# Coefficients of four groups at once on GpSimd, normalisation 6:2, every fourth mask on ScalarE, weights loaded behind x's first tile, matmuls on zeros in TensorE's gaps

## What is computed

```
h   = relu((x - mean) / sqrt(var + 1e-5))            x: [128 graphs, 128 nodes, 128]
out = 0
for each direction (fwd, bwd, loop):
    p = h @ W.T;  g = p @ Wg.T
    vals_r = (p + b_r) * sigmoid(g + bg_r)           for each relation r of the direction
    out   += sum_r (adj == r) @ vals_r               (adj transposed for bwd and loop)
result = x + relu(out)
```

## Time and profile before

| | us |
|---|---|
| median of three runs | 113.24 |
| lowest, highest | 112.27, 114.36 |
| profiled execution | 112.11 |
| its span | 110.3 |
| busy in the span: TensorE, VectorE, ScalarE, GpSimd | 98.8, 94.0, 91.8, 87.1 |

### The profile page before, as it was taken

One profiled execution on the slowest core, in us unless ns is written; L12 is line 12 of the kernel. 1 busy time (PEld: TensorE's weight loads), 2 busy tenths in 40 slices (PEclk: granted clock), 3 DMA queues, 4 the chain that ended last, 5 costly groups with the idle time before them and its releaser, 6 DMA issues.

```text
span 110.3 us, 2526 instructions
## 1 busy us (share of the span) xinstructions
PE 98.8 (90%) x780; PEld 92.1 (83%) x780; DVE 94.0 (85%) x202; ACT 91.8 (83%) x153; POOL 87.1 (79%) x182
## 2 busy tenths in 40 slices
PE   5524789899999999999999999999999999999970
PEld 1113569789999999999999999999999999999960
DVE  1508529899999999999999999999999999897780
ACT  4137533999999999999999999999999999999650
POOL 2380790999999999999999999999999999995000
PEclk9999999999999999999999999999999999999999
DMA  2999999999999999999999999980606050515067
GB/s 73 281 311 281 286 290 291 292 291 292 291 317 311 343 332 321 320 320 321 305 320 301 260 309 274 317 222 6 190 6 190 6 180 10 158 38 176 14 185 207
DMA packets 50275, 25.48 MB, mean 231 GB/s; under 512 B 850, under 2 KB 50260, under 8 KB 50260
## 3 DMA queue, kind: packets, MB, share of 16 engines
q1 hardware_dynamic: 49968, 25.17, 81.6%
q10 hardware_dynamic: 292, 0.13, 0.5%
HBM read 16.91 MB, written 8.39 MB: 229 GB/s over the span
## 4 chain that ended last, share of the span: by engine, by line
PE 80%; DMA 5%; POOL 3%; DVE 3%; issue 2%; ACT 2%; ACTq 1%; DVEq 0%; POOLq 0%
PE psum L750 23%; PE psum L715 16%; PE psum L728 14%; PE psum L729 13%; PE psum L733 13%; DMA w_raw<-in_L_gnn_Wg_loop 5%; POOL rstd L309 1%; DVE x_all L560 1%; DVE stats L500 1%; POOL xn L324 1%; PE psum L691 1%; ACT xn L393 1%; ACT hT_hi L404 1%; ACT L374 1%; PE psum L688 0%
## 5 line engine op out<-in xcount | busy, mean ns | idle before, releaser
L728 PE MATMUL psum<-w_hi,hT_hi 128*128 128x256 f32 x128 | 35.1, 307 | 1.8 <-issue 0.8
L750 PE MATMUL psum<-vals,mask 128*128 128x128 f32 x256 | 33.6, 275 | 0.0
L411 ACT ACTIVATE psum<-bias_all 128x1024 f32<-128x1024 f32 x32 | 32.9, 1027 | 0.1
L324 POOL TENSOR_SCALAR xn<-x_all,mean_neg,rstd 128x128 f32<-128x128 f32 x75 | 32.8, 449 | 0.1
L729 PE MATMUL psum<-w_lo,hT_hi 128*128 128x256 f32 x128 | 32.4, 285 | 0.0
L750 PEld LDWEIGHTS psum<-vals,mask 128*128 128x128 f32 x256 | 31.2, 191 | 0.1
L728 PEld LDWEIGHTS psum<-w_hi,hT_hi 128*128 128x128 f32 x128 | 24.7, 193 | 2.8 <-issue 1.7
L309 POOL TENSOR_TENSOR rstd<-var_eps,minus_half 128x8 f32<-128x8 f32 (+1 forms) x17 | 26.6, 1564 | 0.0
L500 DVE BATCH_NORM_STATS2 stats<-x_all 128x6 f32<-128x256 f32 x64 | 23.9, 416 | 2.7 <-DMA x_all<-in_x 2.7
L535 DVE TENSOR_TENSOR vals<-psum,gate 128x512 f32<-128x512 f32 (+1 forms) x33 | 21.7, 659 | 4.3 <-ACT gate L426 4.2
L729 PEld LDWEIGHTS psum<-w_lo,hT_hi 128*128 128x128 f32 x128 | 24.8, 193 | 0.0
(11 more groups left out here) (34 smaller groups left out, 34.2 us busy)
## 6 DMA issues: line engine op xcount, KB each, us to landing
adj_all<-in_adj SPq DMA_DIRECT2D x16, 512.0 KB, 6.6
x_all<-in_x SPq DMA_DIRECT2D x15, 512.0 KB, 6.7
out<-x_all SPq DMA_DIRECT2D x15, 512.0 KB, 4.4
x_all<-in_x SPq DMA_DIRECT2D x2, 256.0 KB, 3.1
out<-x_all SPq DMA_DIRECT2D x1, 256.0 KB, 2.5
out<-x_all SPq DMA_DIRECT2D x2, 128.0 KB, 2.5
w_raw<-in_L_gnn_W_loop ACTq DMA_DIRECT2D x1, 64.0 KB, 3.2
w_raw<-in_L_gnn_Wg_loop ACTq DMA_DIRECT2D x1, 64.0 KB, 5.3
```

What stands on the lines that cost most here:

```text
L324: last = pool.tensor_scalar(xn[:, s, j * D:j * D + D], x_all[:, g * GC + j * D:g * GC + j * D + D], mean_neg[:, p, k:k + 1], rstd[:, p, k: ...
L411: nc.scalar.activation(prod_ps[s].rearrange("p g a d -> p g (a d)"), bias_all[:, :, :].rearrange("p a d -> p (a d)").unsqueeze(1) .to_broa ...
L728: nc.tensor.matmul(to, hi, w_hi[:, :], start=False, stop=False, skip_group_check=True)
L750: last = nc.tensor.matmul(to[:, j * D:j * D + D], mask[:, g % MASKS, j * N:j * N + N], vals[:, s, j * D:j * D + D], start=True, stop=True)
```

## The change

- Coefficients: `BATCHES` says which groups get theirs together: group 0, group 1, groups 2 and 3, 4 and 5, then four groups at a time from 6 on (16 columns). The slots for statistics and coefficients are four. shift is gone, and VectorE's tiles take the mean straight from the statistics (subtract, then multiply).
- Normalisation: ScalarE has no share. GpSimd has three tiles of each group and VectorE one (in the first two groups one and three), so 6 and 2 of the eight tiles of two groups.
- Masks: groups 0, 1 and every g with g % 4 == 3 are cast on ScalarE, in the loop two before; the others on GpSimd as before.
- Loads: W_loop and Wg_loop are issued from SP's queue right behind x's first group.
- TensorE: `keep_busy` makes matmuls on zeros, 16 in all, at five places of the start.
- VectorE: output before normalise in a loop; row_stats of group t+8 instead of t+6, so groups 7 and 8 are done before the loops too; normalise(0) stands ahead of the splitting of the weights.
- ScalarE's start: seed(0) stands ahead of the second half of w_hi, seed(1) behind relu_turned(0), the masks of groups 0 and 1 behind relu_turned(1).
- The store of the first half of the last group is issued from ScalarE.

```diff
+    BATCHES = [(0, 0), (1, 1), (2, 3), (4, 5)] + [(g, min(g + 3, GROUPS - 1)) for g in range(6, GROUPS, 4)]
+    BATCH = 4 * GROUP
...
-        def shares(g):
-
-            if g < 2:
-                return range(0), range(0, 2), range(2, 4)
-            if g % 2 == 0:
-                return range(0, 3), range(3, 4), range(4, 4)
-            return range(0, 2), range(2, 3), range(3, 4)
-
-        def act_norms(g):
-
-            return g + 1 if g < 2 else 2 + (g - 1) // 2
+        def batch_of(g):
+
+            for b, (first, last) in enumerate(BATCHES):
+                if first <= g <= last:
+                    return b, first, last
+
+        def pool_share(g):
+
+            return 1 if g < 2 else 3
+
+        def mask_by_act(g):
+            return g < 2 or g % MASKS == MASKS - 1
+
+        def masks_before(g, by_act):
+            return sum(mask_by_act(k) == by_act for k in range(g))
...
             load_tile(x_all, x, 0, 0, GROUP, x_first)
+            sp.dma_start(w_raw[:, 0, :], W_loop).then_inc(w_loaded, 16)
+            sp.dma_start(w_raw[:, 1, :], Wg_loop).then_inc(w_loaded, 16)
             load_tile(x_all, x, GROUP, GC, CG - GROUP, x_loaded[0])
             load_x(1)
             load_x(2)
...
-            sp.wait_ge(half_out, 1)
-            store_tile((GROUPS - 1) * GROUP, (GROUPS - 1) * GC, GROUP // 2)
             sp.wait_ge(out_ready, GROUPS)
             store_tile(B - GROUP // 2, (B - GROUP // 2) * D, GROUP // 2)
...
-            def coefficients(p, lo, hi, var_done, pow_done, at, done):
-
-                st = stats[:, p, lo // 2:hi // 2, :].rearrange("p k (e f) -> p k e f", e=2)
-                pool.tensor_scalar(var_eps[:, p, lo:hi].rearrange("p (k e) -> p k e", e=2), st[:, :, :, 2],
-                                   1.0 / D, EPS, ALU.mult, ALU.add).then_inc(var_done, 1)
-                pool.tensor_scalar(mean_neg[:, p, lo:hi].rearrange("p (k e) -> p k e", e=2), st[:, :, :, 1],
-                                   -1.0, 0.0, ALU.mult, ALU.add)
-                pool.wait_ge(var_done, at)
-                pool.tensor_tensor(rstd[:, p, lo:hi], var_eps[:, p, lo:hi], minus_half[:, lo:hi], ALU.pow
-                                   ).then_inc(pow_done, 1)
-                pool.wait_ge(pow_done, at)
-                pool.tensor_tensor(shift[:, p, lo:hi], mean_neg[:, p, lo:hi], rstd[:, p, lo:hi], ALU.mult
-                                   ).then_inc(done, 1)
+            def coefficients(b):
+
+                first, last = BATCHES[b]
+                s, n = b % BATCH_SLOTS, (last - first + 1) * GROUP
+                st = stats[:, s, 0:n // 2, :].rearrange("p k (e f) -> p k e f", e=2)
+                pool.wait_ge(stats_ready, b + 1)
+                if b >= BATCH_SLOTS:
+                    pool.wait_ge(normed_dve, BATCHES[b - BATCH_SLOTS][1] + 1)
+                pool.tensor_scalar(var_eps[:, s, 0:n].rearrange("p (k e) -> p k e", e=2), st[:, :, :, 2],
+                                   1.0 / D, EPS, ALU.mult, ALU.add).then_inc(var_ready, 1)
+                pool.wait_ge(var_ready, b + 1)
+                pool.tensor_tensor(rstd[:, s, 0:n], var_eps[:, s, 0:n], minus_half[:, 0:n], ALU.pow
+                                   ).then_inc(rstd_ready, 1)
+                pool.tensor_scalar(mean_neg[:, s, 0:n].rearrange("p (k e) -> p k e", e=2), st[:, :, :, 1],
+                                   -1.0, 0.0, ALU.mult, ALU.add).then_inc(mean_ready, 1)
             def normalise(g):
-                s, p = g % XN, g // CHUNK % 2
-                if g % CHUNK == 0:
-                    pool.wait_ge(coef_ready, g // CHUNK + 1)
+                b, first, _ = batch_of(g)
+                if g == first:
+                    pool.wait_ge(rstd_ready, b + 1)
+                    pool.wait_ge(mean_ready, b + 1)
                 if g >= XN:
                     pool.wait_ge(turned, g - XN + 1)
-                for j in shares(g)[0]:
-                    k = g % CHUNK * GROUP + j
+                for j in range(pool_share(g)):
+                    k = (g - first) * GROUP + j
                     last = pool.tensor_scalar(
-                        xn[:, s, j * D:j * D + D], x_all[:, g * GC + j * D:g * GC + j * D + D],
-                        mean_neg[:, p, k:k + 1], rstd[:, p, k:k + 1], ALU.add, ALU.mult)
+                        xn[:, g % XN, j * D:j * D + D], x_all[:, g * GC + j * D:g * GC + j * D + D],
+                        mean_neg[:, b % BATCH_SLOTS, k:k + 1], rstd[:, b % BATCH_SLOTS, k:k + 1],
+                        ALU.add, ALU.mult)
                 last.then_inc(normed_pool, 1)
...
             def edges(g):
-                if g % CHUNK == 0:
-                    pool.wait_ge(adj_loaded[g // CHUNK], 16)
+                pool.wait_ge(adj_loaded[g // CHUNK], 16)
                 if g >= MASKS:
                     pool.wait_ge(summed, g - (MASKS - 1))
                 pool.tensor_copy(mask[:, g % MASKS, :], adj_all[:, g * GC:g * GC + GC]
                                  ).then_inc(mask_ready, 1)
-            def chunk_coefficients(c):
-
-                pool.wait_ge(stats_ready, c + 1)
-                if c >= 2:
-                    pool.wait_ge(normed_dve, (c - 1) * CHUNK)
-                    pool.wait_ge(normed_act, act_norms((c - 1) * CHUNK - 1))
-                coefficients(c % 2, GROUP if c == 0 else 0, CG, var_ready, pow_ready, c + 1, coef_ready)
-
-            pool.wait_ge(first_stats, 1)
-            coefficients(0, 0, GROUP, first_var, first_pow, 1, first_coef)
-            chunk_coefficients(0)
-            chunk_coefficients(1)
+            coefficients(0)
+            normalise(0)
+            coefficients(1)
+            normalise(1)
+            coefficients(2)
             normalise(2)
-            edges(0)
             normalise(3)
             for t in range(GROUPS):
-                if t % CHUNK == 0 and live(t + 4):
-                    chunk_coefficients((t + 4) // CHUNK)
-                if live(t + 1):
+                if live(t + 4) and batch_of(t + 4)[1] == t + 4:
+                    coefficients(batch_of(t + 4)[0])
+                if live(t + 1) and not mask_by_act(t + 1):
                     edges(t + 1)
                 if live(t + 4):
                     normalise(t + 4)
...
-            act.dma_start(w_raw[:, 0, :], W_loop).then_inc(w_loaded, 16)
-            act.dma_start(w_raw[:, 1, :], Wg_loop).then_inc(w_loaded, 16)
-
-            def normalise(g):
-
-                s, p = g % XN, g // CHUNK % 2
-                if not shares(g)[2]:
-                    return
-                if g == 0:
-                    act.wait_ge(first_coef, 1)
-                else:
-                    act.wait_ge(coef_ready, g // CHUNK + 1)
-                if g >= XN:
-                    act.wait_ge(turned, g - XN + 1)
-                for j in shares(g)[2]:
-                    k = g % CHUNK * GROUP + j
-                    last = nc.scalar.activation(
-                        xn[:, s, j * D:j * D + D], x_all[:, g * GC + j * D:g * GC + j * D + D], ACT.Identity,
-                        bias=shift[:, p, k:k + 1], scale=rstd[:, p, k:k + 1])
-                last.then_inc(normed_act, 1)
+
+            def edges(g):
+
+                act.wait_ge(adj_loaded[g // CHUNK], 16)
+                if g >= MASKS:
+                    act.wait_ge(summed, g - (MASKS - 1))
+                nc.scalar.activation(mask[:, g % MASKS, :], adj_all[:, g * GC:g * GC + GC], ACT.Copy
+                                     ).then_inc(mask_act, 1)
...
+            act.wait_ge(w_turned, 1)
+            nc.scalar.activation(w_gT[:, :], bank[6][:, 128:256], ACT.Copy).then_inc(w_gT_ready, 1)
+            nc.scalar.activation(w_hi[:, 0:D], bank[6][:, 0:D], ACT.Copy).then_inc(w_hi_ready, 1)
             act.wait_ge(bits_set, 1)
             act.wait_ge(bias_ready, 1)
             seed(0)
-            act.wait_ge(w_turned, 1)
-            nc.scalar.activation(w_gT[:, :], bank[6][:, 128:256], ACT.Copy).then_inc(w_gT_ready, 1)
-            nc.scalar.activation(w_hi[:, 0:D], bank[6][:, 0:D], ACT.Copy).then_inc(w_hi_ready, 1)
             act.wait_ge(w_turned, 2)
             nc.scalar.activation(w_hi[:, D:2 * D], bank[7][:, 0:D], ACT.Copy).then_inc(w_hi_ready, 1)
-            normalise(0)
+            relu_turned(0)
             seed(1)
-            act.wait_ge(half_ready, 1)
-            relu_turned(0)
-            normalise(1)
             sigmoid(0)
             relu_turned(1)
+            edges(0)
+            edges(1)
+            act.wait_ge(half_ready, 1)
             for t in range(GROUPS):
-                if live(t + 3):
-                    normalise(t + 3)
                 if live(t + 2):
                     relu_turned(t + 2)
                     seed(t + 2)
@@ -461,6 +444,13 @@
                     sigmoid(t + 1)
                 if t % CHUNK == 0:
                     watch(t // CHUNK)
+                if live(t + 2) and mask_by_act(t + 2):
+                    edges(t + 2)
```

(50 more changed lines are left out.)

44 lines of the change are left out of this document (16 added, 28 removed).

## The result

The changed kernel takes 107.34 us (median, 106.95 to 107.69) where the kernel before takes 113.54 in the same runs: ratio 0.950, 95% interval 0.944 to 0.955. That is faster by more than 2%, inside the range 104.3 to 110.0, and 0.6 us above the forecast of 106.7. Its profiled execution took 107.37 us with a span of 105.6; that of the kernel before took 112.11, 110.3. So the profiled time fell by 4.7 us and the median by 6.2. The working of the forecast was made against the profiled one and came to 6.5; its sum was 1.8 us too large. The median came out near by luck: the one profiled execution of the kernel before lay 1.0% under the median of its first three runs, and that of the changed kernel lies on its own. Where the same kernel's executions lie over 1.5% above its fastest, the ratios leave them out.

The account below looks back on a forecast made before the run. GpSimd was taken as the bound, at 5.71 us for two groups. Gains of 4.1 (start), 2.1 (steady stretch) and 0.3 (end) sum to 6.5 us, from 113.24 to 106.7; range 104.3 to 110.0.

Parts of the forecast that it names:

- four groups 10.6: GpSimd, steady stretch: four groups fall from 11.42 us to 10.6 (9.4 to 11.0), so it stops being the bound.
- TensorE's floor is 11.02 for four groups: TensorE, steady stretch: its own work is 5.51 us for two groups, 11.02 for four, without waits for GpSimd.
- VectorE's 11.12: VectorE, steady stretch: floor 10.84 plus 0.28 for one normalisation of four meeting a cast; gain 2.1 us in all.
- Batches late: not the bound, 0.6 to spare: Steady loop: despite late first rows, the product beginning the next set can start at 10.4, before 11.0.
- The rival with 0.5 us in each of seven batches: Each batch's first group makes TensorE wait 0.5 us, 3.5 in all: 110.2 us; chance 6%.
- The hold by the power: Rival: GpSimd's power holds VectorE's normalisation, a loop 1.9 us longer, 12.7 for four groups: 117.8 us; chance 4%.
- the row of 12.91: Profile row before the change: two tiles on VectorE took 0.59 us beside GpSimd's power, not stretched; hold costed at nothing.
- The start: Weights from SP's queue let transposes start at 4.94, first sums at 13.5, 5.3 us earlier; net gain 4.1.
- slow pace: Rival at the start: fills don't lift TensorE's pace before group 0's products, 1.7 us lost: 108.4 us; chance 14%.
- The 1.2 us given back: VectorE at the start: three row statistics before group 1's product, where one stood, lose 1.2 us (0.5 to 2.0).
- The end: Last stores: one moves from SP's queue to ScalarE's, so the last starts earlier by 0.3 us (0 to 0.4).
- The signs named in advance: Trace signs for the forecast, such as first transpose near 5 us, and for its being wrong, such as four groups taking 11.4.

Follow-up runs that it names:

- the short power: The changed kernel with GpSimd's power for each batch of four groups cut to the first 4 of 16 columns; 105.70 us, 0.942 of the kernel before.

## Why the forecast was right, and where it wasn't

**GpSimd: right, to the term.** Power of 16 columns 2.88 forecast, 2.90 measured; block 3.5, measured 3.65; four groups 10.6, measured 10.7 and 10.5 (10.97 from one block to the next less 0.27 of wait, and 11.56 less 1.05). It stopped being the bound in the plain sense.

**"TensorE's floor is 11.02 for four groups": wrong term.** It was read as 5.71 less the waits for GpSimd. With work queued up TensorE does 2.69 a group, 10.8. The floor of VectorE, 10.84, was right (10.88 in the run with the short power), and so VectorE, not TensorE, sets the lowest time that any run reached with VectorE's work whole.

**VectorE's 11.12: mechanism half right, size off.** I forecast one meeting with a cast in four groups at 0.28. It is one in eight, at 0.45, plus 0.25 for a late gate (0.1 of it ahead of hT_lo, for hT_hi) and 0.08 in small gaps; together 22.54 for eight groups, 11.27 for four. The gain of the steady stretch still came out: 1.9 us from group 4 to group 28 (68.57 to 66.70), where 24 groups at the forecast rate give 1.8. It is made up otherwise, though: 0.3 in each of the first two sets of eight groups (22.84 to 22.54 in the second), and 1.27 in the last (22.87 to 21.60), in which no batch is late and VectorE has no row statistics left to make from loop 24 on.

**"Batches late: not the bound, 0.6 to spare": wrong, the step that failed.** I closed the loop through TensorE's 2.75 and found slack. But a batch's statistics come at VectorE's pace, GpSimd then needs 3.65 + 1.33, and TensorE, quicker than either, is ready before that. Every second batch makes TensorE wait 0.8 us. The product that I checked, which begins the next set, was in time: the gate of group 13 ended at 51.48 and the product started at 51.59. The one after it was not, 0.25 late at 54.56: from the late rows to its gate ScalarE makes a relu, a seed, the gate of group 13, a watch, a relu and a seed without a pause, and the closing of the loop had counted only one gate of ScalarE's work. Watch moved out of that loop wasn't tried. The rival with 0.5 us in each of seven batches had the right place; I gave it 6%. What it costs is not 3.5 us, as TensorE makes most of it up. By the trace the pause is 0.25 for each late batch; starting the batch 0.6 us sooner gave 1.4 between groups 0 and 28, shorter holds included.

**The hold by the power: right to reject.** 0.34 us inside the power at 55.76, as the row of 12.91 had said; in all runs together 124 normalisations lay wholly inside a power, at 0.32 to 0.37. The Trainium skill ("SBUF — State Buffer", section "Who interferes with whom") has a VectorE operation in a 2-port mode and a GpSimd operation exclude each other for the whole instruction, whichever starts first. The trace agrees that a cast (61.25) and a tile of GpSimd hold a normalisation (see the last section), though one held for the whole instruction would end 0.34 us behind it and this one ends 0.08 behind. It disagrees for the power, which is what the rival needed.

**The start: places right, 1.2 us too early.** Transposes 4.94 forecast, 5.07 measured. Turned rows 7.2 and 7.54: x's second part was 1.0 us later, not 0.5, and held VectorE. First sums 13.5 and 14.64: I took the fast pace from the turned rows on, and it came at 10.56, in the middle of the products. Hence gained 4.1 rather than 5.3. The fills cost nothing that shows, as forecast: group 0's products begin at 8.88 without them and between 8.86 and 9.74 in the runs with the same loads and fills. Their worth was put at 1.7 (the rival "slow pace"); without them the kernel loses 1.8 to 2.6 us. The 1.2 us given back is right in size: 4.1 at group 0, 3.0 at group 4. But only 0.5 of it is there by group 3 (28.12 before, 24.53 changed); the other 0.6 comes with group 4's sums, behind the late rows of group 6.

**What isn't shown.** No run took back the batches of four or the 6:2 division, so what each is worth in the 1.9 us is open; all masks on GpSimd gave back 0.6 of it (67.33 from group 4 to 28). At the start the weights' place (2.7) and the fills (2.3) come to more than the 4.1 gained at group 0, so they don't simply add.

**The end: 0.3 forecast, nothing measured.** The last store starts 0.3 sooner and lands 0.3 to 0.5 later, because another store is under way.

In sum on the profiled time: start 3.0 for 4.1, steady stretch 1.9 for 2.1, end -0.2 for 0.3.

**The signs named in advance.** The transposes near 5 us, the low products of group 0 at 0.47 (10.92 to 11.40, where the next turned rows start), the power at 2.9 and the short normalisations (seven of eight) came. First sums near 13.5, four groups in 11.0 to 11.2 (11.27) and no wait of TensorE for GpSimd did not. One sign of being wrong came too: group 1's product after 18 us. It started at 18.15, in a profile whose start says nothing below 1 us.

## What to carry to other kernels

When the bound engine is relieved in a lump (one long block instead of two short ones), ask not only whether its total fits but who waits for the first product of the block: two neighbouring lines swapped so that the block starts 0.6 us sooner were worth about 1.4 us by the profiles, where the whole steady gain of the change is 1.9. An engine's floor is not its present period less its recorded waits; read it from a stretch where it has work queued. And where TensorE starts cold with idle gaps, matmuls on zeros in those gaps are worth measuring by themselves: here 1.8 to 2.6 us of 6.2. Take the pace from the spacing of the matmuls there, not from the clock column.

## What the runs showed of the hardware that I hadn't expected

- VectorE's normalisation (a tensor_scalar of 128 columns from and to the state buffer) takes 0.34 us alone and 0.34 inside GpSimd's power of 2.90. Where it begins inside a cast or a tile on GpSimd it can be held to the end of that instruction or of the next: all 93 that took over 0.40 us, in all runs, began inside a cast or a tile and ended 0.08 to 0.11 after the end of one. When another follows without a gap the hold goes on through it: 0.79 and, through a tile and two casts, 1.60 us. In the changed kernel the end of a cast and a tile do it at 86.30, on VectorE and on GpSimd:

```profile
86.30 0.55 DVE L507 TENSOR_SCALAR xn<-x_all,stats,rstd 128x128 f32<-128x128 f32 x1
```

```profile
86.33 1.30 POOL L329 TENSOR_SCALAR xn<-x_all,mean_neg,rstd 128x128 f32<-128x128 f32 x3
```

  The first of the three tiles ends at about 86.77 (1.30 / 3 = 0.43), the normalisation at 86.85. I had read the cost as 0.28 a meeting; in the steady stretches of these runs it goes from 0 to 0.66 by the phase.
- The clock column reads 1.00 for a stretch of which the trace has no record. The record begins at 10.56, 13.56, 15.99 and 17.55 us (changed, weights on ScalarE's queue, before, no fills), and in each of the three where matmuls run just then their spacing falls there, from 0.21 to 0.11 or 0.12 us.
- TensorE has two paces once the record reads 1.00: a group takes 2.74 or 2.75 us in the first one or two loops after a wait and 2.69 or 2.70 from then on. Why is open.
- The power on GpSimd is linear in the columns: 1.03, 1.64 and 2.90 us for 4, 8 and 16, which is 0.39 + 0.157 a column.
- Two loads of 64 KB issued from ScalarE's queue at 1.61 and 2.01 us, beside SP's loads, let the first transpose start at 7.69; issued from SP's queue at 1.25 and 1.78, behind the first load of x, they let it start at 5.07.
